# Context squares spread over two earlier waits of ScalarE; in the one-choice expert layer, gating of one token half runs among the first-layer matmuls of the other

## The reference, cut to what matters

```python
aa = jnp.sum(a * a, axis=-1)[:, None]
D = jnp.sqrt(jnp.maximum(aa + bb - 2.0 * ab, 0.0))
```

```python
gates = softmax(xf @ Wg + bg);  idx = argmax(gates)
h = gelu(einsum('th,ehi->tei', xf, W1) + b1)
y = einsum('tei,eih->teh', h, W2) + b2
out = take_along_axis(y, idx)          # the chosen expert's row alone
```

## Time and profile before

| | |
|---|---|
| three runs | 1147.94, 1148.4, 1153.13 us |
| the profiled execution: its own time | 1149.63 us |
| its span (first to last instruction) | 1147.8 us |
| TensorE matmul busy | 921.1 us, 80% |
| VectorE busy | 687.4 us, 60% |
| ScalarE busy | 478.2 us, 42% |
| mean granted TensorE clock | 0.834 of 2.4 GHz |

### The profile page before, as it was taken

The page is one execution under the profiler, slowest core; times in us unless marked ns, Lnnn a source line. Parts: engine busy times, 40 slices in busy tenths (PEclk is TensorE's granted clock), DMA queues, the critical chain, the costliest instruction groups (busy, mean ns, idle before and its releaser), DMA issues. The chain is left out here.

```text
span 1147.8 us, 16903 instructions
## 1 busy us (share of the span) xinstructions
PE 921.1 (80%) x5997; PEld 565.0 (49%) x6000; DVE 687.4 (60%) x2636; ACT 478.2 (42%) x1123; POOL 2.4 (0%) x15
## 2 busy tenths in 40 slices
PE   5999999499999999996788873466921579499798
PEld 3666666345665665665455543122410432366447
DVE  3656555656656566565555518999999453554232
ACT  3655555455555555553224446112332152213340
POOL 0000000000000000000000000000000000000000
PEclk8999999689999999998568986678755687657578
DMA  8720000000000000000000000000000000000000
GB/s 232 139 50 2 1 1 1 0 1 1 1 1 1 1 1 1 1 1 1 1 1 1 2 1 2 1 1 1 1 0 1 1 1 0 1 1 1 1 0 19
DMA packets 25459, 13.59 MB, mean 12 GB/s; under 512 B 13081, under 2 KB 23713, under 8 KB 25378
## 3 DMA queue, kind: packets, MB, share of 16 engines
q1 hardware_dynamic: 25378, 12.52, 4.5%
HBM read 11.99 MB, written 0.52 MB: 11 GB/s over the span
## 5 line engine op out<-in xcount | busy, mean ns | idle before, releaser
L437 ACT ACTIVATE wide_probs<-PS,wide_nmax 128x512 f32<-128x512 f32 (+2 forms) x256 | 140.4, 557 | 49.8 <-DVE wide_nmax L362 49.8
L362 DVE TENSOR_REDUCE wide_nmax<-PS 128x2 f32<-128x1024 f32 (+2 forms) x128 | 113.7, 888 | 36.5 <-PE PS L307 25.9
L307 PE MATMUL PS<-wide_kT,wide_qT 64*128 64x512 f32 (+2 forms) x512 | 112.8, 518 | 1.9 <-ACT wide_kT L431 1.9
L320 PE MATMUL PS<-constants,wide_probs 128*128 128x128 f32 x704 | 101.6, 278 | 0.0
L285 PE MATMUL PS<-wide_pT,wide_v 128*64 128x256 f32 (+1 forms) x768 | 90.2, 370 | 0.2 <-DVE wide_v L357 0.2
L320 PEld LDWEIGHTS PS<-constants,wide_probs 128*128 128x128 f32 x704 | 78.2, 141 | 18.8 <-ACT wide_probs L437 11.7
L443 ACT COPY wide_pT<-PS 128x512 f32<-128x512 f32 (+2 forms) x128 | 57.8, 451 | 45.4 <-PE PS L320 45.4
L1496 PE MATMUL PS<-w_up_or_diagonal,constants 128*128 128x512 f32 (+2 forms) x44 | 30.5, 785 | 46.6 <-DVE w_up_or_diagonal L1636 46.6
L368 DVE COPY wide_pT<-PS 128x512 f32<-128x512 f32 (+2 forms) x128 | 66.2, 517 | 2.7
L285 PEld LDWEIGHTS PS<-wide_pT,wide_v 128*64 128x64 f32 x768 | 49.9, 136 | 29.1 <-issue 10.4
L383 DVE TENSOR_TENSOR wide_attT<-PS,wide_inverse_spread 128x256 f32<-128x256 f32 x64 | 27.2, 425 | 60.3 <-PE PS L285 59.3
(11 more groups left out here) (420 smaller groups left out, 1779.1 us busy)
## 6 DMA issues: line engine op xcount, KB each, us to landing
ctx_by_lane<-ctx_dram SPq DMA_DIRECT2D x4, 256.0 KB, 7.9
top_w<-L_ffn_W_dram SPq DMA_DIRECT2D x2, 512.0 KB
constants<-constants_dram SPq DMA_DIRECT2D x1, 679.0 KB, 5.7
x<-x_dram SPq DMA_DIRECT2D x1, 512.0 KB, 4.5
l0x_wq<-L_xattn_Wq_dram SPq DMA_DIRECT2D x1, 512.0 KB, 9.2
l0x_wk<-L_xattn_Wk_dram SPq DMA_DIRECT2D x1, 512.0 KB, 5.0
l0x_wv<-L_xattn_Wv_dram SPq DMA_DIRECT2D x1, 512.0 KB, 7.2
l0x_bv<-L_xattn_bv_dram SPq DMA_DIRECT2D x1, 512.0 KB, 5.3
```

Source lines behind the costliest of these rows:

```text
L307: mm = pe.matmul(PS[:, self.S[qt][h], 0:self.keys(qt)], w.qT[rows, n % 2, qt * P:qt * P + P], w.kT[rows, n % 2, 0:self.keys(qt)], start=Tr ...
L320: mm = pe.transpose(PS[:, self.T[h], kt * P:kt * P + P], w.probs[:, qt, h, kt * P:kt * P + P], ident)
L362: v.tensor_reduce(w.nmax[:, (2 * n + qt) % 4, :], PS[:, self.S[qt][0]:self.S[qt][1] + 1, 0:self.keys(qt)], AX.X, ALU.max, negate=True).the ...
L437: act.activation(w.probs[:, qt, h, 0:self.keys(qt)], PS[:, self.S[qt][h], 0:self.keys(qt)], ACT.Exp, bias=w.nmax[:, (2 * n + qt) % 4, h:h ...
```

## The change

1. `scalar_aa` takes a range. Squares 0 to 7 are issued at the end of stage 0, after ScalarE's last work there and ahead of its meet; squares 8 to 15 in stage 1, after yT's copies and ahead of the mix's first Relu. The scratch is a tile of its own, `square`. Nothing is left of them in stage 2.
2. First-layer results go to four banks in turn (3, 6, 7, 0), and step i waits for the Gelu of step i - 4 (step 3, which overwrites bank 0, waits for VectorE's reading of the router's product).
3. The one-hot is copied once, to bfloat16. Each of the first-layer steps 8 to 15 is followed by spread i - 8, and VectorE gates tokens 0 to 511 while TensorE does the first layer of tokens 512 to 1023. Spreads 8 to 15 stand in pairs ahead of output tiles 0 to 3.
4. The bias b2 is split into three bfloat16 parts by five VectorE operations of 8x128 ahead of the router's work (`vector_bias`). The bias of a tile is then three bfloat16 matmuls in place of one float32 matmul.
5. The output leaves in two DMAs of 256 KB, each after VectorE's addition of its half; SyncE no longer waits for the meet.

```diff
-    def scalar_aa(self, act):
-        for p in range(self.LANES):
-            act.activation(self.k.yT[:, 0:D], self.k.ctxP[:, p, :], ACT.Square, accum_out=...).then_inc(self.aa_sb, 1)
-            act.wait_ge(self.aa_sb, p + 1)
+    def scalar_aa(self, act, first, last):
+        for p in range(first, last):
+            if p:
+                act.wait_ge(self.aa_sb, p)
+            act.activation(self.k.square[:, :], self.k.ctxP[:, p, :], ACT.Square, accum_out=...).then_inc(self.aa_sb, 1)
...
+        def hidden(i):
+            if i == 3:
+                pe.wait_ge(self.by_v, 1)
+            if i >= 4:
+                pe.wait_ge(self.by_a, i - 4 + 2)
+            pe.matmul(PS[:, self.HID[i % 4], :], self.w1[:, i % NE, :], k.yT[:, half(i // NE)], ...).then_inc(self.product, 1)
+        def spread(i):
+            if i >= 2:
+                pe.wait_ge(self.by_v, self.v_gated(i - 2))
+            pe.matmul(PS[:, self.SPREAD[i % 2], :], k.identb[0:NE, ...], self.ohb[:, half(i // NE)], ...).then_inc(self.product, 1)
         def output(t):
-            pe.matmul(out, self.ohT[:, t * P:t * P + P], self.b2[:, :], start=True, stop=False)
+            for i in range(3):
+                pe.matmul(out, self.ohb[:, t * P:t * P + P], self.b2_parts[:, i, :], start=(i == 0), stop=False)
             for e in range(NE):
                 mm = pe.matmul(out, self.h[:, e, t * P:t * P + P], self.w2[:, e, :], ...)
...
+        for i in range(NE):
+            hidden(i)
+        pe.wait_ge(self.by_v, self.V_OH)
+        for t in range(TILES):
+            mm = pe.transpose(PS[0:NE, self.SPREAD[t // 4], ...], self.oh[:, t, :], k.ident)
+        mm.then_inc(self.product, 1)
+        for i in range(NE):
+            hidden(NE + i)
+            if i == 0:
+                pe.wait_ge(self.by_v, self.V_OH + 1)
+            spread(i)
+        pe.wait_ge(self.bias_parts, 5)
+        for t in range(TILES):
+            if t < 4:
+                spread(NE + 2 * t)
+                spread(NE + 2 * t + 1)
+            if t % 4 == 0:
+                pe.wait_ge(self.by_v, self.v_gated(2 * t + NE - 1))
+            mm = output(t)
...
+        v.tensor_copy(parts[:, 0, :], self.b2[:, :])
+        v.tensor_tensor(rest[:, :], self.b2[:, :], parts[:, 0, :], ALU.subtract)
+        v.tensor_copy(parts[:, 1, :], rest[:, :])
+        v.tensor_tensor(rest[:, :], rest[:, :], parts[:, 1, :], ALU.subtract)
+        v.tensor_copy(parts[:, 2, :], rest[:, :])
...
-            sp.wait_ge(k.stage_done, 4 * 8)
-            sp.dma_start(out.rearrange("b (t p) d -> p (b t) d", p=P), k.x[:, :, :]).then_inc(out_done, 16)
+            for f in range(2):
+                sp.wait_ge(l3f.x_done, f + 1)
+                sp.dma_start(out[2 * f:2 * f + 2].rearrange(...), k.x[:, 4 * f:4 * f + 4, :]).then_inc(out_done, 16)
...
             l0x.scalar(act)
+            act.wait_ge(ctxP_in, 64)
+            l2x.scalar_aa(act, 0, 8)
             k.meet(act, 0)
...
             ln.scalar_yT(act, 1)
+            l2x.scalar_aa(act, 8, l2x.LANES)
             l0f.scalar(act)
...
             ln.scalar_std(act, 2)
-            act.wait_ge(ctxP_in, 64)
-            l2x.scalar_aa(act)
             ln.scalar_yT(act, 2)
```

More of the change, by code:

```diff
@@ L2130, in tensor @@
         half = lambda f: slice(f * BANK, f * BANK + BANK)
+        def hidden(i):
[3 more added lines that the diff above has]
+                pe.wait_ge(self.by_a, i - 4 + 2)
+            pe.matmul(PS[:, self.HID[i % 4], :], self.w1[:, i % NE, :], k.yT[:, half(i // NE)], start=True, stop=True).then_inc(self.product, 1)
+        def spread(i):
+            if i >= 2:
+                pe.wait_ge(self.by_v, self.v_gated(i - 2))
+            pe.matmul(PS[:, self.SPREAD[i % 2], :], k.identb[0:NE, i % NE:i % NE + 1].to_broadcast((NE, P)), self.ohb[:, half(i // NE)],
+                      start=True, stop=True).then_inc(self.product, 1)
@@ L2138, in output @@
             if t % 4 == 3:
                 mm.then_inc(self.product, 1)
[L2142 to L2161, removed]
@@ L2162, in tensor, with v_gated @@
-        pe.wait_ge(self.by_v, self.V_OH + 2 + self.STEPS)
-        for t in range(4, TILES):
-            output(t)
+    def v_gated(self, i):
+        return self.V_OH + 2 + i
     def scalar(self, act):
@@ L2172, in scalar @@
             act.wait_ge(self.product, self.p_hidden(i))
-            act.activation(self.h[:, i % 8, (i // 8) * BANK:(i // 8) * BANK + BANK], PS[:, (3, 6)[i % 2], :], ACT.Gelu,
+            act.activation(self.h[:, i % 8, (i // 8) * BANK:(i // 8) * BANK + BANK], PS[:, self.HID[i % 4], :], ACT.Gelu,
                            bias=self.b1[:, i % 8:i % 8 + 1]).then_inc(self.by_a, 1)
@@ L2216, in vector, with add @@
         v.wait_ge(self.product, self.P_OH)
-        for dst in (self.ohT, self.ohb):
-            done(v.tensor_copy(dst[:, :].rearrange("p (f c) -> p f c", f=2), PS[0:NE, 1:3, :]))
+        done(v.tensor_copy(self.ohb[:, :].rearrange("p (f c) -> p f c", f=2), PS[0:NE, self.SPREAD[0]:self.SPREAD[1] + 1, :]))
+        x = self.k.x
+        def add(f):
+            v.wait_ge(self.product, self.p_out(f))
+            r = slice(4 * f, 4 * f + 4)
+            v.tensor_tensor(x[:, r, :], x[:, r, :], PS[:, self.OUT[f], :].rearrange("p (t d) -> p t d", t=4), ALU.add).then_inc(self.x_done, 1)
         for i in range(self.STEPS):
@@ L2222, in vector, with vector_bias @@
             h = self.h[:, i % 8, (i // 8) * BANK:(i // 8) * BANK + BANK]
-            done(v.tensor_tensor(h, h, PS[:, 1 + i % 2, :], ALU.mult))
-        x = self.k.x
+            done(v.tensor_tensor(h, h, PS[:, self.SPREAD[i % 2], :], ALU.mult))
         for f in range(2):
-            v.wait_ge(self.product, self.p_out(f))
-            r = slice(4 * f, 4 * f + 4)
-            v.tensor_tensor(x[:, r, :], x[:, r, :], PS[:, 4 + f, :].rearrange("p (t d) -> p t d", t=4), ALU.add)
+            add(f)
+    def vector_bias(self, v):
+        parts, rest = self.b2_parts, self.b2_rest
+        v.wait_ge(self.loaded, self.n_loads)
+        v.tensor_copy(parts[:, 0, :], self.b2[:, :]).then_inc(self.bias_parts, 1)
+        v.wait_ge(self.bias_parts, 1)
+        v.tensor_tensor(rest[:, :], self.b2[:, :], parts[:, 0, :], ALU.subtract).then_inc(self.bias_parts, 1)
+        v.wait_ge(self.bias_parts, 2)
+        v.tensor_copy(parts[:, 1, :], rest[:, :]).then_inc(self.bias_parts, 1)
+        v.wait_ge(self.bias_parts, 3)
+        v.tensor_tensor(rest[:, :], rest[:, :], parts[:, 1, :], ALU.subtract).then_inc(self.bias_parts, 1)
+        v.wait_ge(self.bias_parts, 4)
+        v.tensor_copy(parts[:, 2, :], rest[:, :]).then_inc(self.bias_parts, 1)
 def build(nc, a, cst_d, out):
```

22 lines of the change are left out of this document (15 added, 7 removed).

## The result

| | kernel before | changed kernel |
|---|---|---|
| first measurement | 1147.94, 1148.40, 1150.32, 1153.13 us | 1137.92, 1138.03, 1138.59, 1155.19, 1160.96, 1162.03 us |
| ratio | | 0.9898, 95% interval 0.9867 to 0.9929 |
| again (first experiment) | 1146.3 us, median of 24 | 1132.99, 1133.82, 1133.95, 1134.27, 1139.49, 1156.03 us |
| ratio | | 0.9895, 95% interval 0.9863 to 0.9927 |

With all of them counted, the six runs of the first measurement have a median of 1146.9 us, against 1149.4 for the four of the kernel before. The ratios say 11.7 us and 12.0 us less, against a forecast of 10.8.

The account below looks back on a forecast made before the run. No engine is full throughout, so waits bound the kernel: squares ahead of yT's copies, VectorE's gating (also lowering TensorE's clock), the store. -4.3 - 5.6 - 0.9 = -10.8 us from the median 1148.4 gives 1137.6; range 1133.0 to 1142.5.

Parts of the forecast that it names:

- Squares, -4.3: Start of stage 2: without sixteen squares ahead of yT's second copy, it ends at 226.7 instead of 231.02 us, 4.3 us gained.
- both covers: Stages 0 and 1: eight squares each fit in ScalarE's waits, with 1.4 us to spare at the meet and 2.0 at the Relu.
- the far bound of 2.4 us: Stages 0 and 1: largest cost if Square needs a table load of its own; the forecast took 0.
- Expert layer, -5.6: Last layer: gating laid beside the first layer, four banks, one cast and bfloat16 bias end it at 1137.8 against 1143.4 us.
- I take 0.05, since the 512-column matmul gives time to load weights under it: First-layer steps with spreads: type changes add 0.05 us a step, bounds 0 to 0.2, making 1.18 instead of 1.13.
- the rival's 0.4 to 0.6: Expert layer: type change costs 0.4 to 0.6 us a step, 3 to 5 in all, 1140.6 to 1142.6 us; chance 0.12.
- The recorded sign of being right: Expert layer: new first-layer steps 1.1 to 1.25 us apart at clock 1.00, one of several signs listed.
- the sign of being wrong: Expert layer: a first-layer step over 1.4 us, listed beside a 0.50 clock after the router and table loads at the squares.
- Output tiles: Expert layer: tiles with spreads take 2.69 us, those without 2.30; bias in three bfloat16 matmuls gives 0.6 us in all.
- Banks, -0.4: First half of the first layer: with four banks the Gelu waits go, and the transposes end at 1107.1 instead of 1107.5 us.
- Overlap and clock: Expert layer: about 6.1 us of gating laid beside other work, and 2.0 us of the output tile at the low clock saved.
- Store, -0.9: Final output: the second half of 256 KB takes half the DMA time, 0.9 us less, bounds nothing to 1.2.

Follow-up runs that it names:

- first experiment: The changed kernel run once more, unchanged, against the kernel before: six runs from 1132.99 to 1156.03 us, ratio 0.9895.
- The pairs: Changed kernel with spreads two at a time behind every second first-layer step: ratio 0.9921; with all tiles' bias matmuls in one block as well, 0.9883.
- their own experiment: Changed kernel with first-layer results in banks 3 and 6 alone, each step waiting for the Gelu of step i - 2: one profiled run, 1159.53 us.
- the left columns: Columns of a dropped table of time by stage: the kernel before, profiled at 1149.63 us, and the unchanged changed kernel, profiled at 1133.95 us.
- the lower group: The faster of two groups, some 20 us apart, of the changed kernel's runs: 1137.92 to 1138.59 us in the first measurement; the upper 1155.19 to 1162.03.

## Why the prediction was right, and where it was off

- **Squares, -4.3: right** in the wait (5.02 to 0.67 us) and in both covers. The table load behind the squares was to be done 0.17 us before it was wanted; it was done 0.76 us before. No table load was added, so the far bound of 2.4 us played no part. By the Trainium skill (ScalarE: Activation LUTs, "What ACT_TABLE_LOAD costs") a switch would have cost 2.66 us; no run here has one for a Square, and the loads that there are take 1.28 us, the next activation right behind (203.06 after the load at 201.77). Of the 4.35 us stage 2 kept 3.4, or 5.3 to 5.9 in three profiles: the clock's share, for which the forecast had plus or minus 1.7.
- **Expert layer, -5.6: the mechanism was right, one term too small in cost.** It gave 4.4. The step that failed is "I take 0.05, since the 512-column matmul gives time to load weights under it": a mixed step took 1.37 us and not 1.18, 1.3 us over seven steps. That is 0.24 over the 1.13 of the separate rows, beyond the forecast's own bound of 0.2 and short of the rival's 0.4 to 0.6. The chain shows 1.05 for the two first-layer matmuls where 0.86 had been, and 0.32 for the spread where 0.27 had been. The pairs, with half the changes, show that the changes cost it and not the waits. The row that the forecast took for the price of a change of type (0.41 against 0.22) is that of a change from 128 weight rows to 8 within float32. The first spread came another 0.2 us late and took 0.1 longer. The recorded sign of being right, steps 1.1 to 1.25 us apart, was missed; the sign of being wrong, over 1.4, was not reached.
- **Output tiles: slightly better than forecast.** 0.53 + 0.17 + 1.98 = 2.68 and 0.27 + 1.98 = 2.25, for 2.69 and 2.30. The tiles give back 0.4 us of it. The bias parts are worth 0.7 us, forecast 0.6.
- **Banks, -0.4: right.** 7.4 to 7.0 us at 2.4 GHz by their own experiment.
- **Overlap and clock:** right; taking the overlap out costs 4.6 us, 3.5 of it two tiles at 3.71.
- **Store, -0.9: too large.** From the end of the last add to the end of the span were 3.68 us in both profiles with one store. With two stores seven of twelve profiles have 2.73 or 2.74, the other five 3.2 to 4.9; the median gain is the forecast 0.94, the mean 0.5. The stretch of the transfer halved, the time to its end varies.
- **Sum:** by terms -4.35 - 4.4 - 0.5 to 0.9 = -9.3 to -9.7 us. The measured -11.7 and -12.0 are more than that, and intervals of 7 us hold both. What is left over is not in the terms; between the two profiles of the left columns it lies in stages 0, 3, 5 and 6. That the forecast of 10.8 is nearer to the measured ratio than its terms are is luck.
- **What the prediction did not have:** that with a stage moved by 4 us the clock of later stages can come out differently, for tens of microseconds. It looked for the clock only in stages 2 and 7. Its range, 1133.0 to 1142.5 us, holds the lower group but for one run at its edge (1132.99) and nothing of the upper one, and with all six first runs taken together the median of 1146.9 us would be what it called no change. None of the rivals named this.

## What to carry to other kernels

Laying one engine's chain beside another's first layer is worth its microseconds twice where the wait had also let TensorE's clock fall, and a reordering that saves 1 us of work can spend it again by opening such a wait (the pairs). In a stream of matmuls count the changes of the number of weight rows: from 128 to 8 and back cost about 0.3 us here, among matmuls of 512 columns (2.74 us for two steps, 2.44 with one such change less) as among those of 128 (a tile with its bias 2.25 us, 1.83 + 0.17 = 2.00 apart). A change of type with the rows kept showed no cost. Where the granted clock changes within stages, compare stretch by stretch: the same program came out 20 us apart by the clock of stages in which nothing had been edited.

## What the runs showed of the hardware

- The granted clock in a stage was not a property of the stage. The same 1023 matmuls of stage 3 ran at a mean of 0.77, 0.73, 0.72 or 0.68 of 2.4 GHz and took 157.8, 164.4, 164.8 or 172.2 us; 162.0 and 178.4 us were seen once each. Which of these a profile has goes with the time from the stage's start to the clock's first fall, to a few tenths of a microsecond, in all fourteen. Stages 0 and 1 themselves end up to 4 us apart from run to run.
- A stage where TensorE is busier is not one with a higher clock: in stage 3 it was busy 142.84 of 172.20 us at a mean of 0.68, and 125.73 of 157.80 at 0.77, since the same matmuls last longer at the low clock. Its score matmuls stand as 19*128 in the trace, 19 of 128 rows; whether that is why the clock stays low was not tried.
- A change of weight rows from 128 to 8 cost a float32 bias of two passes 0.19 us (0.41 for 0.22) and one of three bfloat16 passes 0.10 (0.27 for 0.17); a change of type from bfloat16 to float32 with 8 rows kept showed none.
- Twenty memsets of 128x6 in a row took 0.6 us on VectorE, 0.03 us each.
